# Filler products in TensorE's waits and four output buffers, in the tail of an attention and expert kernel

## The chip, the cores and the metric

One core of a Trainium2 chip. The metric is the device time of one execution in microseconds (us). The engines are TensorE (PE, its weight loads PEld), VectorE (DVE), ScalarE (ACT), GpSimd (POOL) and SyncE (SP), which issues DMAs.

## The reference

For 8 sequences of 512 tokens with 128 features: a modulated layer norm, causal attention with 16 heads and relative positions, a gated residual; then a second modulated layer norm and a layer of 16 experts, in which each token goes to one:

```python
x = x + ga * attention(layernorm(x) * (1 + ca) + sa)
h = (layernorm(x) * (1 + cb) + sb).reshape(-1, 128)
score = softmax(h @ Wg + bg)
gate, idx = max(score), argmax(score)
pos = rank of the token among those of its expert, in token order
keep = pos < 256                          # 4096 tokens / 16 experts
buf[idx, pos] = h                         # kept tokens alone
y = relu(buf @ W1 + b1) @ W2 + b2         # expert by expert
x = x + gb * where(keep, y[idx, pos] * gate, 0)
```

## The kernel before

Attention runs over 64 steps (8 sequences by 8 pairs of heads), one order written out by hand for each engine; the engines meet only at semaphores. A sequence's way into the experts lies inside the steps of the next one. For the last sequence it has no cover, and stands behind the steps as the tail: `project_out` (L729), the residual (`hn`, L1014), `turn_a` (transposes, L737), the layer norm of VectorE and GpSimd, `turn_h` (transposes, L744), ScalarE's `h2T`, `logits` (L750), the choice of the expert on VectorE, `places` (ranks by products, L757 to L762), indices, and four scatters of rows by GpSimd into a buffer in DRAM (L359). Each of these steps waits for the one before. A row of that buffer holds the token's normed values, its residual, its gate and its number (3 x 128 + 1 floats).

Meanwhile SyncE has loaded the weights of eight experts. It then waits for the scatters and loads the rows of experts 0 to 3 into four slots. From there on it waits for `ym` (TensorE done with expert e) and loads the weights of expert e + 8, and for `y` (output e summed) and loads the rows of expert e + 4.

TensorE does, for each expert e: `hidden(e)` (12 products with 256 columns, L850, on a high and a low part of both operands), `turn_e(e + 1)` (two transposes, L841) and `down(e)` (16 product instructions, L861, tile 0 and then tile 1 of 128 tokens, both in bank 6 or 7). `hidden(0)` needs `xhi` of ScalarE and `xlo` of VectorE (`low_x`). ScalarE does two of an expert's four relus, VectorE the other two (L1205).

VectorE's order for expert e is: `relu(e)`, `low_x(e + 1)`, `output(e - 1)`, `low_w1(e + 2)` (the low part of the weights, L1192). `output` waits until the scatter of the expert two before has left its buffer (`ysc`), converts the token numbers to indices (`yidx`, L1213), waits for `ym`, and sums: bias (L1217), times gate (L1219), plus residual (L1220), over both tiles at once. There are two output buffers, halves of the tile `row`. GpSimd then scatters the two tiles of each expert's output to their tokens (L414). Ahead of the experts, VectorE waits for the scatters of L359 and for the biases, and then does `low_w1` of experts 0 and 1 and `low_x(0)`.

In the names, `bank` is a bank of PSUM; `prb[0]` is bank 4, last read ahead of the last `weighted` (L722). `wohi` is the output projection's weight.

Of the kernel before, what the change touches and what calls it, by code (L numbers as in the profile page):

```python
# [32 lines left out]
U32 = mybir.dt.uint32  # L33
ALU = mybir.AluOpType
# [3 lines left out]
P = 128  # L38
B, S, D = 8, 512, 128
# [5 lines left out]
E, FF = 16, 512  # L45
# [25 lines left out]
def program(nc, x_d, qkv_d, qb_d, pos_d, wo_d, bo_d, wg_d, bg_d, w1_d, b1_d, w2_d, b2_d, c_d, wmod_d,  # L71
            consts_d, ktab_d, out_d):
    ctx = ExitStack()
    with ctx:
        def sb(name, shape, dt=F32):
            return ctx.enter_context(nc.sbuf_tensor(name, shape, dt))

        def sem(name):
# [86 lines left out]
        ye = row[:, :, 0:D].rearrange("p (a t) d -> p a t d", a=2)  # L165
        yidx = sb("yidx", [P, 2, ST], U32)
# [14 lines left out]
                 "xl0 xl1 xl2 xl3 w0 w1 w2 w3 w4 w5 w6 w7 w1h w1l tx xt xl hm hr hh2 ym y yi ysc0 ysc1").split()  # L181
# [18 lines left out]
        def waits(eng, *pairs):  # L200

            for name, value in pairs:
                wait(eng, name, value)

        def batches(turn):

            for b in range(B):
                turn(b, b == 0, b == B - 1)
# [5 lines left out]
        def one(tile, b, *rest):  # L214

            return tile[(slice(None), bass.ds(b, 1)) + rest]

# [4 lines left out]
        def _(sp):  # L222
# [72 lines left out]
            for e in range(E - 4):  # L295
                if e < E - 8:
                    sp.wait_ge(s["ym"], e + 1)
                    load_w1(e + 8, e)
                    load_w2(e + 8, e)
                sp.wait_ge(s["y"], e + 1)  # L300
                rows(e + 4, e % 4)
# [3 lines left out]
        def _(gp):  # L305
# [105 lines left out]
            def expert(e, par):  # L411
                waits(gp, ("pch", 1), ("y", e + 1), ("yi", e + 1))
                for t in range(ST):
                    gp.indirect_dma_start(out=out_d.rearrange("b s d -> (b s) d"),  # L414
                                          out_offset=bass.IndirectOffsetOnAxis(ap=yidx[:, par, t:t + 1], axis=0),
                                          in_=ye[:, par, t, :], in_offset=None,
                                          bounds_check=B * S - 1, oob_is_err=False).then_inc(s[f"ysc{par}"], 16)

            for e in range(E):
                expert(e, e % 2)  # L420
            for par in range(2):
                gp.wait_ge(s[f"ysc{par}"], 16 * ST * E // 2)
# [180 lines left out]
        def _(pe):  # L603
# [129 lines left out]
            def turn_a(b):  # L733

                pe.wait_ge(s["ga"], b)
                for q in range(QT):
                    last = pe.transpose(xtb[:, q * P:(q + 1) * P], hn[:, q * P:(q + 1) * P], ident)  # L737
                last.then_inc(s["t_a"], 1)
# [84 lines left out]
            pe.wait_ge(s["kt"], 4)  # L823
            batches(turn)
# [3 lines left out]
            weighted(NJ - 1, PAIRS - 1, NJ, 3)  # L828
            project_out(NJ - 1, PAIRS - 1)
            turn_a(B)  # L830
            pe.wait_ge(s["x2"], B)
            turn_h(B)
            logits(B)
            pe.wait_ge(s["lge"], B)
            places(B)

# [17 lines left out]
            def down(e, r):  # L854

                pe.wait_ge(s["hh2"], 2 * e + 1)
                for t in range(ST):
                    for n in range(NB):
                        if t == 0:
                            pe.wait_ge(s["hr" if n % 2 == 0 else "hh2"], 2 * e + n // 2 + 1)  # L860
                        last = pe.matmul(bank[6 + r % 2][:, t * P:(t + 1) * P], hid[:, r % 2, n, t * P:(t + 1) * P],  # L861
                                         w2[:, r, n, :], start=(n == 0), stop=(n == NB - 1))
                last.then_inc(s["ym"], 1)
# [17 lines left out]
        def _(dve):  # L881
# [326 lines left out]
            def output(e, r, first=False):  # L1208
                par = r % 2
                if not first:  # L1210
                    dve.wait_ge(s[f"ysc{par}"], 16 * (e - par))

                dve.tensor_copy(yidx[:, par, :], slots[:, r, :, 3 * D]).then_inc(s["yi"], 1)  # L1213
                dve.wait_ge(s["ym"], e + 1)

                rows = ye[:, par, :, :]
                link(dve.tensor_tensor(rows, bank[6 + par][:, 0:CAP].rearrange("p (t d) -> p t d", t=ST),  # L1217
                                       one(b2, e, slice(None)).to_broadcast([P, ST, D]), ALU.add))
                link(dve.tensor_tensor(rows, rows, slots[:, r, :, 2 * D:3 * D], ALU.mult))  # L1219
                dve.tensor_tensor(rows, rows, slots[:, r, :, D:2 * D], ALU.add).then_inc(s["y"], 1)  # L1220

            dve.wait_ge(s["scat"], 64 * B)
            dve.wait_ge(s["b2"], 16)
            for e in range(2):
                low_w1(e, e)
            low_x(0, 0)

            def expert(e, r, first=False):

                par = r % 2  # L1230
                relu(e, par)
                if e + 1 < E:
                    low_x(e + 1, 1 - par)
                if e:
                    output(e - 1, (r - 1) % 4, first)
                if e + 2 < E:
                    low_w1(e + 2, par)

            for e in range(E):
                expert(e, e % 4, e < 3)  # L1240
            output(E - 1, 3)


# [41 lines left out]
```

## Time and profile before

| | |
|---|---|
| median of 3 runs | 917.59 us (914.37, 918.48, 917.59) |
| profiled execution | 917.26 us, span 915.2 us |
| mean granted clock of TensorE | 0.972 |
| busy: PE, PEld | 94%, 75% of the span |
| busy: DVE, ACT, POOL | 73%, 78%, 57% of the span |
| chain of waits | PE 88%, DVE 5%, DMA 2%, ACT 2% |

A granted clock of 1.00 is 2.4 GHz, and 0.50 is 1.2 GHz. The span runs from the first to the last instruction. The attention steps end at about 812 us, the first rows are loaded at 839.9, the last scatter starts at 907.2. In a timeline a row can stand for several instructions of one kind (x4), and the time given is that of all of them; a product's time includes its way through the array, so that one starts before the last has ended.

### The profile page before, as it was taken

To read this page: it belongs to the slowest core of one execution; us is meant where nothing else is said; L and a number is where in the kernel's file an instruction comes from. 1 tells how busy PE (TensorE), PEld (TensorE's weight loads), DVE (VectorE), ACT (ScalarE), POOL (GpSimd) and SP (SyncE) were. 2 spreads that over 40 slices of the span, in tenths; PEclk is the share of its full clock that TensorE was granted. 3 is DMA by queue.
4 is the path that set the end of the run, shared out by engine and by line. 5 is a ranking of instruction groups with operands and counts; after the bars stand their busy time and mean duration, and the time that the engine had idled before them with its cause. 6 is when DMAs were issued, how large, how long until landed. Compare 5 with 4: busy or idle time off the path is not lost.

```text
span 915.2 us, 17265 instructions
## 1 busy us (share of the span) xinstructions
PE 857.6 (94%) x5453; PEld 686.8 (75%) x5453; DVE 667.8 (73%) x2051; ACT 710.9 (78%) x1966; POOL 519.6 (57%) x783
## 2 busy tenths in 40 slices
PE   5799999999999999999999999999999999963994
PEld 4577778777777787777777787777777877732994
DVE  5677778786878778777878787868787686743784
ACT  3688888888888888888888888888888888831441
POOL 3355555666556755675557556665567556732454
PEclk8899999999999999999999999999999999985997
DMA  8059000000000000000000000000000000025761
GB/s 247 1 163 257 19 1 13 1 1 36 13 2 1 36 1 13 1 19 17 13 1 15 12 14 1 1 21 12 2 1 21 1 13 1 13 72 165 224 196 39
DMA packets 31130, 38.43 MB, mean 42 GB/s; under 512 B 2982, under 2 KB 25703, under 8 KB 30784
## 3 DMA queue, kind: packets, MB, share of 16 engines
q1 hardware_dynamic: 27488, 29.69, 11.5%
q0 software_dynamic: 3072, 5.94, 1.8%
q10 hardware_dynamic: 480, 1.70, 0.5%
q8 instruction: 44, 0.72, 0.3%
q14 instruction: 46, 0.38, 0.1%
HBM read 22.97 MB, written 16.82 MB: 43 GB/s over the span
## 4 chain that ended last, share of the span: by engine, by line
PE 88%; DVE 5%; DMA 2%; ACT 2%; issue 1%; POOL 1%; SPq 0%; POOLq 0%; DVEq 0%
PE bank L694 22%; PE bank L659 16%; PE bank L722 16%; PE bank L702 15%; PE bank L729 5%; PE bank L680 5%; PE bank L691 3%; PE bank L861 2%; PE bank L850 2%; DMA out<-row,yidx 1%; ACT prob L493 1%; PE bank L750 1%; DVE xn L930 1%; DMA small<-in_L_ffn_b 1%; PE bank L744 0%
## 5 line engine op out<-in xcount | busy, mean ns | idle before, releaser
L373 POOL TENSOR_SCALAR prob<-prob,rsum 128x128 f32<-128x128 f32 (+3 forms) x512 | 263.7, 534 | 238.1 <-DVE rsum L987 233.6
L493 ACT ACTIVATE prob<-srow,nmax 128x512 f32<-128x512 f32 (+3 forms) x512 | 286.2, 560 | 66.7 <-DVE nmax L975 64.0
L975 DVE CUSTOM_DVE_ANT_0 srow<-bank,consts 128x512 f32<-128x512 f32 (+3 forms) x512 | 246.7, 489 | 100.0 <-issue 78.6
L702 PE MATMUL bank<-consts,prob 128*128 128x128 f32 x1280 | 201.9, 272 | 0.2 <-POOL prob L373 0.2
L702 PEld LDWEIGHTS bank<-consts,prob 128*128 128x128 f32 x1280 | 158.6, 140 | 23.3 <-POOL prob L373 0.5
L366 POOL TENSOR_TENSOR qlo<-qx,qhi 128x384 fp32r<-128x384 f32 x128 | 129.9, 1015 | 58.1 <-ACT qhi L482 57.3
L502 ACT ACTIVATE pt<-bank 128x384 f32<-128x384 f32 x318 | 153.6, 496 | 5.5 <-PE bank L702 5.0
L722 PE MATMUL bank<-pt,v 128*64 128x512 f32 (+3 forms) x1024 | 152.0, 439 | 0.2 <-issue 0.2
L694 PE MATMUL bank<-khi,qhi 128*128 128x512 f32 (+2 forms) x384 | 145.9, 380 | 5.9 <-DVE wolo L1175 2.4
L992 DVE SCALAR_TENSOR_TENSOR qx<-bank,qbias,consts 128x512 f32<-128x512 f32 x128 | 94.1, 735 | 53.6 <-PE bank L659 53.4
L694 PE MATMUL bank<-khi,qlo 128*128 128x512 f32 (+2 forms) x384 | 130.2, 339 | 0.0
L694 PE MATMUL bank<-klo,qhi 128*128 128x512 f32 (+2 forms) x384 | 128.9, 336 | 0.0
L722 PEld LDWEIGHTS bank<-pt,v 128*64 128x64 f32 x1024 | 68.0, 136 | 76.8 <-issue 59.6
L998 DVE SCALAR_TENSOR_TENSOR klo<-bank,khi 64x512 fp32r<-64x512 f32 x128 | 87.8, 686 | 18.9 <-ACT kx L477 16.8
L493 ACT ACTIVATION_READ_ACCUMULATOR prob<-srow,nmax 128x1 f32 x512 | 97.5, 191 | 0.0
L482 ACT ACTIVATE qhi<-qx 128x384 fp32r<-128x384 f32 x128 | 66.6, 520 | 38.1 <-DVE qx L992 37.6
L659 PE MATMUL bank<-hhi,whi 128*128 128x512 f32 x189 | 86.5, 458 | 1.0 <-DVE qx L992 0.9
L694 PEld LDWEIGHTS bank<-khi,qhi 128*128 128x128 f32 x384 | 72.2, 188 | 19.6 <-issue 6.9
L694 PEld LDWEIGHTS bank<-klo,qhi 128*128 128x128 f32 x384 | 72.8, 190 | 7.7
L476 ACT ACTIVATE khi<-bank 64x512 fp32r<-64x512 f32 x128 | 75.2, 588 | 2.7 <-PE bank L659 1.2
L694 PEld LDWEIGHTS bank<-khi,qlo 128*128 128x128 f32 x384 | 72.2, 188 | 5.4
L659 PE MATMUL bank<-hhi,wlo 128*128 128x512 f32 x189 | 74.7, 395 | 0.0
(166 smaller groups left out, 1388.4 us busy)
## 6 DMA issues: line engine op xcount, KB each, us to landing
xbuf<-fill SPq DMA_DIRECT2D x4, 1540.0 KB, 23.2
x<-xbuf SPq DMA_DIRECT2D x16, 385.0 KB, 3.4
raw<-in_L_ffn_W SPq DMA_DIRECT2D x16, 256.0 KB, 8.7
prob<-in_L_ffn_W SPq DMA_DIRECT2D x16, 256.0 KB, 4.8
out<-row SPq DMA_DIRECT2D x8, 256.0 KB, 2.3
raw<-in_L_attn_qkv ACTq DMA_DIRECT2D x3, 512.0 KB, 5.9
modb<-mod_rows SPq DMA_DIRECT2D x1, 1536.0 KB, 8.1
v<-in_L_ffn_b SPq DMA_DIRECT2D x1, 1024.0 KB, 6.9
```

Of the source, the lines that this page charges most:

```text
L366: gp.tensor_tensor(qlo[:, h, :], qx[:, h, P:S], qhi[:, h, :], ALU.subtract).then_inc(s["ql"], 1)
L373: end = gp.tensor_scalar(part, part, rsum[:, par, 4 * h + q:4 * h + q + 1], 1.0, ALU.mult, ALU.mult)
L476: act.activation(khi[0:HD, h, :], prb[0][h * HD:(h + 1) * HD, :], ACT.Copy, scale=C_QKV)
L493: act.activation(prob[:, par, h, QOFF[q]:QOFF[q] + P * (q + 1)], srow[:, k % 4, 0:P * (q + 1)], ACT.Exp, bias=nmax[:, par, k:k + 1], scale ...
L502: act.activation(pt[:, h, KOFF[g]:KOFF[g] + GW[g]], source[:, 0:GW[g]], ACT.Copy)\
L659: last = pe.matmul(out, w[:, a, cols], h, start=(i == 0), stop=(i == 2))
L694: last = pe.matmul(out, a[:, h, (q - 1) * P:q * P], b[:, h, 0:P * (q + 1)], start=(i == 0), stop=(i == 2))
L702: last = pe.transpose(out[:, n * P:(n + 1) * P], prob[:, par, h, QOFF[q] + k * P:QOFF[q] + (k + 1) * P], ident)
L722: last = pe.matmul(otb[h * HD:(h + 1) * HD, k * P:S], v[:, g, k, at + h * HD:at + (h + 1) * HD], pt[:, h, KOFF[k]:KOFF[k] + S - k * P], st ...
L975: dve.tensor_tensor_reduce(out=srow[:, k % 4, 0:w], in0=scb[k % 2][:, 0:w], in1=mask[:, S - w:S], scale=-1.0, scalar=BIG, op0=ALU.add, op1 ...
L992: dve.scalar_tensor_tensor(qx[:, h, :], prb[h][:, :], qbias[:, h, a:a + 1], qtab, ALU.add, ALU.mult).then_inc(s["qe"], 1)
L998: dve.scalar_tensor_tensor(klo[0:HD, h, :], prb[0][h * HD:(h + 1) * HD, :], C_QKV, khi[0:HD, h, :], ALU.mult, ALU.subtract).then_inc(s["kl ...
```

## The change

The diff adds `idle(n)`: n products of `wohi` with 512 of its own columns into `prb[0]`, without a wait or a signal. They stand in TensorE's order in the tail: 6 before the last `project_out`, 4 before `turn_a`, 14 before `turn_h`, 3 before `logits`, 6 before `places`, 44 behind `places`.

The expert outputs get four buffers (`ye`, two in `row` and two in `xh`), with four scatter semaphores; `output` waits for the scatter of the expert four before. `ym` and `y` are now raised once per tile. GpSimd waits for each tile by itself before it scatters it. `output` can do one tile alone; that of expert 15 is summed and scattered tile by tile, its second tile coming from bank 0 in place of bank 7. `output(14)` stands before `relu(15)`, no longer behind it. `low_w1` of experts 0 and 1 stands before the wait for the scatters.

```diff
--- before.py
+++ after.py
@@ -162,8 +162,8 @@
         xf = x[:, :, :].rearrange("p t d -> p (t d)")
         slots = xf[:, 0:4 * ST * RW].rearrange("p (a t w) -> p a t w", a=4, t=ST)
         hid = srow[:, :, :].rearrange("p k s -> p (k s)").rearrange("p (a n c) -> p a n c", a=2, n=NB)
-        ye = row[:, :, 0:D].rearrange("p (a t) d -> p a t d", a=2)
-        yidx = sb("yidx", [P, 2, ST], U32)
+        ye = [row[:, 0:2, 0:D], row[:, 2:4, 0:D], xh[:, 0:2, :], xh[:, 2:4, :]]
+        yidx = sb("yidx", [P, 4, ST], U32)
 
         bank = [ctx.enter_context(nc.psum_tensor(f"bank{i}", [P, 512], F32)) for i in range(8)]
         scb, trb, prb, otb, opb = bank[0:2], bank[2:4], bank[4:6], bank[6], bank[7]
@@ -178,7 +178,7 @@
                  "st1 st2 rst1 rs1 xn t_x hn vhi vlo hld wv qh ql kl kt wos ol ga t_a "
                  "sc tt ex rc nm tr evA evB pv oe qp qe kp ke vp ve op "
                  "dch pch va1 va2 x2 rst2 rs2 xh h2a h2 t_h hh lg lge lm lex oh gate gg pre prx idx scat filled x2st "
-                 "xl0 xl1 xl2 xl3 w0 w1 w2 w3 w4 w5 w6 w7 w1h w1l tx xt xl hm hr hh2 ym y yi ysc0 ysc1").split()
+                 "xl0 xl1 xl2 xl3 w0 w1 w2 w3 w4 w5 w6 w7 w1h w1l tx xt xl hm hr hh2 ym y yi ysc0 ysc1 ysc2 ysc3").split()
         s = {n: sem("s_" + n) for n in names}
 
         class Chain:
@@ -214,6 +214,10 @@
         def one(tile, b, *rest):
 
             return tile[(slice(None), bass.ds(b, 1)) + rest]
+
+        def down_bank(e, t):
+
+            return bank[0] if (e, t) == (E - 1, ST - 1) else bank[6 + e % 2]
 
         block = ctx.enter_context(nc.Block())
 
@@ -294,10 +298,10 @@
                 rows(e, e)
             for e in range(E - 4):
                 if e < E - 8:
-                    sp.wait_ge(s["ym"], e + 1)
+                    sp.wait_ge(s["ym"], ST * (e + 1))
                     load_w1(e + 8, e)
                     load_w2(e + 8, e)
-                sp.wait_ge(s["y"], e + 1)
+                sp.wait_ge(s["y"], ST * (e + 1))
                 rows(e + 4, e % 4)
 
 
@@ -408,18 +412,19 @@
             scatter(B, range(QT))
 
 
-            def expert(e, par):
-                waits(gp, ("pch", 1), ("y", e + 1), ("yi", e + 1))
+            def expert(e, r):
+                waits(gp, ("pch", 1), ("yi", e + 1))
                 for t in range(ST):
+                    gp.wait_ge(s["y"], ST * e + t + 1)
                     gp.indirect_dma_start(out=out_d.rearrange("b s d -> (b s) d"),
-                                          out_offset=bass.IndirectOffsetOnAxis(ap=yidx[:, par, t:t + 1], axis=0),
-                                          in_=ye[:, par, t, :], in_offset=None,
-                                          bounds_check=B * S - 1, oob_is_err=False).then_inc(s[f"ysc{par}"], 16)
+                                          out_offset=bass.IndirectOffsetOnAxis(ap=yidx[:, r, t:t + 1], axis=0),
+                                          in_=ye[r][:, t, :], in_offset=None,
+                                          bounds_check=B * S - 1, oob_is_err=False).then_inc(s[f"ysc{r}"], 16)
 
             for e in range(E):
-                expert(e, e % 2)
-            for par in range(2):
-                gp.wait_ge(s[f"ysc{par}"], 16 * ST * E // 2)
+                expert(e, e % 4)
+            for r in range(4):
+                gp.wait_ge(s[f"ysc{r}"], 16 * ST * E // 4)
 
 
         @block.scalar
@@ -821,18 +826,30 @@
             pe.wait_ge(s["ve"], 3)
             pe.wait_ge(s["ktab"], 48)
             pe.wait_ge(s["kt"], 4)
+            def idle(n):
+
+                for _ in range(n):
+                    pe.matmul(prb[0][:, :], wohi[:, 0, :], wohi[:, 0:4, :].rearrange("p a d -> p (a d)"),
+                              start=True, stop=True)
+
             batches(turn)
             for i in range(6):
                 transpose_group(free[i], NJ - 1, 1, *divmod(i, 3))
             project_out(NJ - 2, PAIRS - 2)
             weighted(NJ - 1, PAIRS - 1, NJ, 3)
+            idle(6)
             project_out(NJ - 1, PAIRS - 1)
+            idle(4)
             turn_a(B)
+            idle(14)
             pe.wait_ge(s["x2"], B)
             turn_h(B)
+            idle(3)
             logits(B)
+            idle(6)
             pe.wait_ge(s["lge"], B)
             places(B)
+            idle(44)
 
 
             def turn_e(r):
@@ -858,9 +875,9 @@
                     for n in range(NB):
                         if t == 0:
                             pe.wait_ge(s["hr" if n % 2 == 0 else "hh2"], 2 * e + n // 2 + 1)
-                        last = pe.matmul(bank[6 + r % 2][:, t * P:(t + 1) * P], hid[:, r % 2, n, t * P:(t + 1) * P],
+                        last = pe.matmul(down_bank(e, t)[:, t * P:(t + 1) * P], hid[:, r % 2, n, t * P:(t + 1) * P],
                                          w2[:, r, n, :], start=(n == 0), stop=(n == NB - 1))
-                last.then_inc(s["ym"], 1)
+                    last.then_inc(s["ym"], 1)
 
             pe.wait_ge(s["prx"], B)
             pe.wait_ge(s["xl0"], 16)
@@ -1205,40 +1222,35 @@
                     dve.tensor_scalar(hid[:, par, n, :], bank[2 + n][:, 0:CAP], smallT[:, bass.ds(16 + NB * e + n, 1)],
                                       0.0, ALU.add, ALU.max).then_inc(s["hh2"], 1)
 
-            def output(e, r, first=False):
-                par = r % 2
-                if not first:
-                    dve.wait_ge(s[f"ysc{par}"], 16 * (e - par))
-
-                dve.tensor_copy(yidx[:, par, :], slots[:, r, :, 3 * D]).then_inc(s["yi"], 1)
-                dve.wait_ge(s["ym"], e + 1)
-
-                rows = ye[:, par, :, :]
-                link(dve.tensor_tensor(rows, bank[6 + par][:, 0:CAP].rearrange("p (t d) -> p t d", t=ST),
-                                       one(b2, e, slice(None)).to_broadcast([P, ST, D]), ALU.add))
-                link(dve.tensor_tensor(rows, rows, slots[:, r, :, 2 * D:3 * D], ALU.mult))
-                dve.tensor_tensor(rows, rows, slots[:, r, :, D:2 * D], ALU.add).then_inc(s["y"], 1)
-
+            def output(e, t0=0, t1=ST):
+                r, width = e % 4, (t1 - t0) * P
+                if t0 == 0:
+                    wait(dve, f"ysc{r}", 32 * (e // 4))
+                    dve.tensor_copy(yidx[:, r, :], slots[:, r, :, 3 * D]).then_inc(s["yi"], 1)
+                dve.wait_ge(s["ym"], ST * e + t1)
+                rows = ye[r][:, t0:t1, :]
+                link(dve.tensor_tensor(rows, down_bank(e, t0)[:, t0 * P:t1 * P].rearrange("p (t d) -> p t d", d=D),
+                                       one(b2, e, slice(None)).to_broadcast([P, t1 - t0, D]), ALU.add))
+                link(dve.tensor_tensor(rows, rows, slots[:, r, t0:t1, 2 * D:3 * D], ALU.mult))
+                dve.tensor_tensor(rows, rows, slots[:, r, t0:t1, D:2 * D], ALU.add).then_inc(s["y"], t1 - t0)
+
+            for e in range(2):
+                low_w1(e, e)
             dve.wait_ge(s["scat"], 64 * B)
             dve.wait_ge(s["b2"], 16)
-            for e in range(2):
-                low_w1(e, e)
             low_x(0, 0)
 
-            def expert(e, r, first=False):
-
-                par = r % 2
-                relu(e, par)
-                if e + 1 < E:
-                    low_x(e + 1, 1 - par)
+            for e in range(E - 1):
+                relu(e, e % 2)
+                low_x(e + 1, 1 - e % 2)
                 if e:
-                    output(e - 1, (r - 1) % 4, first)
+                    output(e - 1)
                 if e + 2 < E:
-                    low_w1(e + 2, par)
-
-            for e in range(E):
-                expert(e, e % 4, e < 3)
-            output(E - 1, 3)
+                    low_w1(e + 2, e % 2)
+            output(E - 2)
+            relu(E - 1, 1)
+            for t in range(ST):
+                output(E - 1, t, t + 1)
 
 
 def host_constants():
```

## Rows read from the trace of the kernel before

**Rows 1.** Stretches: length, busy us (x instructions) of PE, PEld, DVE, ACT, POOL; clock.

```profile
52.30:55.70 3.40, 1.84 (x14) 0.96 (x10) 3.30 (x16) 1.26 (x5) 0.08 (x1) 1.00 0.02 4
813.40:816.80 3.40, 1.61 (x7) 0.90 (x7) 1.50 (x3) 0.00 (x0) 0.00 (x0) 1.00 0.00 0
816.90:821.30 4.40, 0.00 (x0) 0.00 (x0) 2.66 (x13) 0.00 (x0) 1.29 (x2) 0.50 0.69 194
841.70:847.50 5.80, 5.75 (x27) 5.78 (x28) 2.08 (x4) 1.85 (x4) 0.00 (x0) 0.50 0.22 78
```

**Rows 2.** Timeline of the tail: start, us, instruction, count, [idle before it <- releaser].

```profile
813.85 0.50 PE L729 MATMUL bank<-ohi,wohi 128*128 128x512 f32 x1 [1.42 <-DVE olo L1004]
...
815.82 0.66 PE L737 MATMUL bank<-consts,hn 128*128 128x128 f32 x4 [1.00 <-DVE hn L1014]
...
821.34 1.09 PE L744 MATMUL bank<-consts,xh 128*128 128x128 f32 x4 [4.87 <-DVE xh L1037]
823.29 1.89 PE L750 MATMUL bank<-wg,h2T 128*128 128x16 f32 x8 [0.87 <-ACT h2T L512]
826.87 0.21 PE L757 MATMUL bank<-oh,upper 128*128 128x64 bf16 x1 [1.69 <-DVE oh L1061]
...
836.94 1.29 DVE L1192 TENSOR_TENSOR wlo<-raw,whi 128x512 fp32r<-128x512 f32 x2 [7.36 <-DMA xbuf<-row,sidx]
...
840.07 0.66 PE L841 MATMUL bank<-consts,x 128*128 128x128 f32 x2 [12.80 <-DMA x<-xbuf]
841.75 0.55 PE L850 MATMUL bank<-hhi,whi 128*128 128x256 f32 x1 [1.02 <-DVE hlo L1199]
```

**Rows 3.** Timeline of TensorE earlier in the run, both levels of the clock.

```profile
25.62 0.63 PE L659 MATMUL bank<-vhi,whi 128*128 128x512 f32 x1
26.05 0.63 PE L659 MATMUL bank<-vlo,whi 128*128 128x512 f32 x1
...
28.77 0.40 PE L680 MATMUL bank<-wvhi,vlo 128*128 128x512 f32 x1
29.00 0.40 PE L680 MATMUL bank<-wvhi,vhi 128*128 128x512 f32 x1
...
171.05 0.60 PE L744 MATMUL bank<-consts,xh 128*128 128x128 f32 x4
...
182.46 0.96 PE L750 MATMUL bank<-wg,h2T 128*128 128x16 f32 x8
```

**Rows 4.** Timeline of TensorE, first product of experts 1, 6, 7, 10, 11, 15.

```profile
847.87 0.36 PE L850 MATMUL bank<-hhi,whi 128*128 128x256 f32 x1
...
865.25 0.36 PE L850 MATMUL bank<-hhi,whi 128*128 128x256 f32 x1
...
869.71 0.36 PE L850 MATMUL bank<-hhi,whi 128*128 128x256 f32 x1
...
880.31 0.37 PE L850 MATMUL bank<-hhi,whi 128*128 128x256 f32 x1
...
884.78 0.36 PE L850 MATMUL bank<-hhi,whi 128*128 128x256 f32 x1
...
898.72 0.37 PE L850 MATMUL bank<-hhi,whi 128*128 128x256 f32 x1
```

**Rows 5.** Waits behind 845: who for whom, us in total, times, longest us.

```profile
DVE yidx L1213 <- DMA out<-row,yidx: 3.5, 4, 1.4
```

**Rows 6.** Timeline of GpSimd and VectorE at the end.

```profile
900.09 0.97 POOL L414 DMA_INDIRECT out<-row,yidx  x1 [1.14 <-DVE row L1220]
901.36 0.97 POOL L414 DMA_INDIRECT out<-row,yidx  x1 [0.30 <-DVE yidx L1213]
...
903.64 0.45 DVE L1213 CAST yidx<-x 128x2 uint32<-128x2 f32 x1 [1.36 <-DMA out<-row,yidx]
...
907.17 0.97 POOL L414 DMA_INDIRECT out<-row,yidx  x1 [0.30 <-issue]
```

**Rows 7.** VectorE's groups behind 845: count, busy us, mean ns, idle before.

```profile
L1205 DVE TENSOR_SCALAR srow<-bank,smallT 128x256 f32<-128x256 f32 x31 | 14.7, 481 | 5.1 <-PE bank L850 4.7
L1219 DVE TENSOR_TENSOR row<-row,x 128x256 f32<-128x256 f32 x16 | 6.9, 429 | 0.5
```

## Prediction

> **What bounds the kernel now.** I read the table of busy shares first: TensorE is busy 94% of the span and 88% of the chain of waits runs through it, so the attention stage, which the change does not touch, is TensorE's. What the change can move lies behind that stage: about 812 to 915 us. There the windows show the granted clock. It is 1.00 up to 816.8, although TensorE is busy for only 1.61 of the last 3.4 us, 0.50 right behind, and still 0.50 while the first expert runs [rows 1]. The timeline of TensorE shows why: from the last output projection on, each short group of products waits for another engine, 1.42, 1.00, 4.87, 0.87, 1.69 and then 12.80 us, and the chain goes through VectorE, GpSimd and a DMA and back each time [rows 2]. The tail is thus a latency chain with TensorE as one link, and every TensorE link behind 816.9 runs at 1.2 GHz in place of 2.4 GHz. From 841.75 on it is TensorE's again: sixteen experts, one after the other.
>
> All sums are made against the profiled execution: 917.26 us, of which 915.2 is the span. It lies 0.3 us under the median of 917.59; the three runs differ by 4.1 us, nearly as much as I come to forecast.
>
> **Step 1, the filler itself.** At full clock a product with 512 columns starts 0.23 us after the one before (28.77, 29.00), at half clock 0.43 us (25.62, 26.05) [rows 3]. The fillers have this shape, write a bank that nobody reads any more, and wait for nothing. At full clock they are, in order, 6 x 0.23 = 1.4 us into a slot of 1.42; 4 = 0.9 into 1.00; 14 = 3.2 into 4.87; 3 = 0.7 into 0.87; 6 = 1.4 into 1.69; 44 = 10.1 into 12.80 [rows 2]. They all fit, so their cost is nothing, and the cover is those waits. If the cover is gone (half clock) they need 2.6, 1.7, 6.0, 1.3, 2.6 and 18.9 us, and TensorE takes its instructions in order: the next transpose or product is late by the excess, and with it VectorE's routing, the scatters and the rows' DMA.
>
> **Step 2, the links before the rows are loaded.** Four transposes took 1.09 us at 821.34 and 0.60 at 171.05; the eight products of the logits 1.89 at 823.29 and 0.96 at 182.46 [rows 2, 3]. With the clock kept that is 0.5 + 0.9 us earlier, and an estimated 0.15 for the small products of the places: 1.6 in all. Will it be kept? Fall and no fall have a row each. Busy 1.61 of 3.4 us, the clock fell right behind it; busy 1.84 of 3.4 us (52.3 to 55.7), it stayed at 1.00 [rows 1]. In the new tail the leanest stretch is from the end of the fourteen (about 819.5) to the start of the logits (822.8): 1.8 us idle, 0.6 of transposes, 0.7 of filler, and nothing for 0.1. That is nearer to the row behind which it fell. I take the transposes' 0.5 whole, since a fall can hardly come before them, half of the logits' 0.9, and 0.1 of the places': **1.1 us**. The ends: 1.6; and 0 where the clock falls ahead of the logits, since six fillers at half clock (2.6) overrun their slot by 0.9, which eats most of what the transposes gave.
>
> The Trainium skill speaks to this point ("TensorE: Matmul & The Clock Gate", section "Why this matters for your kernels"): what it warns of is one long idle gap between bursts, not a sum of short ones. This trace disagrees: the clock fell at 816.9 behind gaps of only 1.42 and 1.00 us [rows 2]. By the page nothing in the new tail would cost the clock; that is the first rival below.
>
> **Step 3, the first experts.** The last filler ends near 835.6; the rows of expert 0 then land near 838.4 (1.6 us earlier than now). So TensorE idles for some 2.8 us, does two transposes (0.66 now, an estimated 0.4 warm, by the ratio of step 2), and idles for 1.0 again while the two halves of x are made. That is leaner than either row of [rows 1]. So the clock is likely to fall once more, but late, having been full until then, and it comes back during expert 0 or 1. Now it is half for all of 841.7 to 847.5 [rows 1], which costs 6.12 us from the start of expert 0 (841.75) to that of expert 1 (847.87) in place of an undisturbed 3.49 (worked out in step 4): 2.6 us [rows 2, 4]. The ends are 0 and 2.6; no row says when the fall comes, so I take the middle, **1.2 us**, and **0.2** for the transposes.
>
> **Step 4, four output buffers.** From expert 1 to expert 15, 14 intervals take 898.72 - 847.87 = 50.85 us; two are 869.71 - 865.25 = 4.46 and 884.78 - 880.31 = 4.47, the other twelve average 3.49 [rows 4]. In both long ones VectorE stood at the conversion of the indices until the scatter of the expert two before had landed (four such waits, 3.5 us, the longest 1.4 [rows 5]), and behind it stood the relu for which TensorE waits. With four buffers it waits for the expert four before, seven us older. Both stalls go: 8.93 - 6.98 = **1.9 us**. What would be late next is TensorE itself (its intervals are full); the loads of rows and weights are asked for three and eight experts ahead, as now. Ends: 0.9 (one stall comes back, as the queue of loads is as full as before) and 1.9.
>
> **Step 5, the residue products ahead of the scatter wait.** They ran 1.29 us from 836.94, and nobody needed them before 841.75; VectorE had been idle for 7.36 us before [rows 2]. Moved into that idle time they save 0. The cover of both places is the scatters and the load of the rows; without it 1.3 us would be at stake.
>
> **Step 6, the end.** Now the scatter of expert 13 starts at 900.09 and 901.36, one per 1.27 us, and the last one at 907.17, behind an output that waited 1.36 us for its buffer at 903.64 [rows 6]; from there to the end of the span are 8.0 us, which stay. In the new order output 14 (three operations of 0.43) goes before the two relus of expert 15 (0.48 each) [rows 7]: these come 0.7 us later, and so do expert 15's down products, until about 903. Its second tile is then summed by about 904.1. But GpSimd has four scatters behind 901.36, one every 1.27: the last starts at 901.36 + 4 x 1.275 = 906.46, and it, not the sum, is late. Gain 907.17 - 906.46 = **0.7 us**. Ends: if each wait ahead of a single tile costs the 0.8 us that now lie between an output and its scatter, -1.4; if GpSimd were quicker than its rows, the sum would set the end at 905.2, +1.9. Two more semaphores to wait for at the very end and one more signal per expert of TensorE I put at nothing: no row has them as a wait.
>
> **Sum.** 1.1 + 1.2 + 0.2 + 1.9 + 0.7 = 5.1 us; 917.26 - 5.1 = **912.2 us**, 0.6% under the median.
>
> **Rivals.** *A. The clock is kept throughout*: 1.6 + 2.6 + 0.3 + 1.9 + 0.7 = 7.1, so **910.2 us**. For it: between 812 and 836 TensorE is then nearly always busy. Against it: the idle 2.8 + 1.0 us in front of expert 0.
> *B. The filler does nothing for the time*: the clock falls near 822 and is half again where the first experts run; only the buffers and the end are left, 2.6 us, so **914.7 us**. For it: the fall behind a stretch with 1.61 of 3.4 us busy. Against it: the long run of 44 products, as dense as the nine of 25 to 28 us, behind which the clock had risen [rows 3].
> *C. Slower: the fillers run at half clock.* The overruns are 1.1 (fourteen), 0.4 (three), 0.9 (six) and 6.1 us (forty-four): 8.5 us late, less the 2.6 of buffers and end, **923.2 us**. It decides from this point: the forty-four take 10.1 us plus 0.47 for each us at half clock, and fill 12.80 when 5.8 us of them are half; with the 2.4 us of overruns before, the change is a loss from about 6.2 us on. Against it: at 841.75 the clock was back 5.8 us after dense work began, and in the first dense stretch within 4.
> *D. The buffers don't help*, as the stalls come from elsewhere: 1.9 less, **914.1 us**. Against it: the releaser in the row is the scatter's DMA.
>
> **How the numbers follow.** What a measurement of this kernel can tell from no change is about 0.5%, 4.6 us: under 913.0 is faster, over 922.2 slower. Chances: the forecast case (910.8 to 913.9) 0.50, A 0.20, B 0.18, C 0.04, D or a mix of B and D 0.08. The forecast case lies under 913.0 in three of four, so faster is 0.20 + 0.37 = 0.57; same 0.13 + 0.18 + 0.07 = 0.38; slower 0.05, C and some misfortune. The likeliest case has 910.8 to 913.9; for 8 in 10 the range reaches to A less the 1 us by which a median of such runs moves, and to B with the same: 909.2 to 915.7.
>
> **What would show it.** The page's clock row at 1.0 up to about 838 (steps 1, 2); the logits' eight products at 0.96 us; expert 0 to expert 1 between 3.5 and 6.1 us (step 3); no wait for the scatter's DMA at the index conversion and no interval over 4 us (step 4); six last scatters at 1.27 us with no gap (step 6). The prediction is wrong if a filler is still running when its successor's input is there, or if the clock at expert 0 is as it was.

## The result, and the profile after

The changed kernel takes 914.45 us (median of 13 runs, 912.86 to 917.08) against 917.59 us: a ratio of 0.9973 with a 95% interval of 0.9962 to 0.9983. It is 0.27% faster, 2.5 us by the ratio. The forecast was 912.2 us and 5.1 us less. The medians themselves are 3.1 us apart. The time lies inside the forecast range, but the gain is about half of the forecast.

The profiled execution took 913.59 us, 3.7 us less than that of before; its span is 911.8 us. That is one execution, better than the median of its kernel. Its windows over the tail show the length of each stretch, the busy time of PE, PEld, DVE, ACT and POOL, the granted clock, and then the share of the DMA engines and their GB/s:

```profile
816.80:821.20 4.40, 2.73 (x13) 1.93 (x12) 2.61 (x13) 0.00 (x0) 1.29 (x3) 1.00 0.69 198
823.90:827.10 3.20, 3.20 (x16) 2.21 (x16) 1.93 (x10) 1.29 (x3) 1.04 (x1) 0.50 1.17 329
827.30:840.70 13.40, 10.20 (x46) 7.96 (x45) 2.72 (x10) 0.38 (x1) 4.14 (x4) 1.00 0.42 136
840.90:844.20 3.30, 3.30 (x17) 3.30 (x17) 0.97 (x2) 1.26 (x4) 0.00 (x0) 0.50 0.50 178
```

Where the clock was 0.50 from 816.9 to past 847.5 [rows 1], it now falls twice, each time for some 3.4 us: once at 823.8, while the six fillers ahead of the places run, and once at 840.9, just as expert 0 starts. The timeline of TensorE in the tail shows what each fall costs:

```profile
821.19 0.63 PE L749 MATMUL bank<-consts,xh 128*128 128x128 f32 x4 [1.67 <-DVE xh L1054]
...
822.69 1.07 PE L755 MATMUL bank<-wg,h2T 128*128 128x16 f32 x8 [0.17 <-ACT h2T L517]
823.60 2.75 PE L832 MATMUL bank<-wohi 128*128 128x512 f32 x6
826.15 0.28 PE L762 MATMUL bank<-oh,upper 128*128 128x64 bf16 x1
...
826.47 10.61 PE L832 MATMUL bank<-wohi 128*128 128x512 f32 x44
839.14 0.41 PE L858 MATMUL bank<-consts,x 128*128 128x128 f32 x2 [2.07 <-DMA x<-xbuf]
840.68 0.40 PE L867 MATMUL bank<-hhi,whi 128*128 128x256 f32 x1 [1.12 <-DVE hlo L1216]
```

The transposes and the logits run at full clock (0.63 and 1.07 us, where they took 1.09 and 1.89 [rows 2]). Then six fillers take 2.75 us, and the places start only when they have drained, at 826.15; the choice they need was written at 825.30. More than half of the 1.26 us won until then goes there.

The first products of experts 1, 5, 6, 9, 10 and 15 answer to [rows 4]:

```profile
845.65 0.36 PE L867 MATMUL bank<-hhi,whi 128*128 128x256 f32 x1
...
859.75 0.37 PE L867 MATMUL bank<-hhi,whi 128*128 128x256 f32 x1
...
863.59 0.36 PE L867 MATMUL bank<-hhi,whi 128*128 128x256 f32 x1
...
874.18 0.37 PE L867 MATMUL bank<-hhi,whi 128*128 128x256 f32 x1
...
878.10 0.36 PE L867 MATMUL bank<-hhi,whi 128*128 128x256 f32 x1
...
895.80 0.37 PE L867 MATMUL bank<-hhi,whi 128*128 128x256 f32 x1
```

Expert 0 takes 845.65 - 840.68 = 4.97 us, 1.15 less. Experts 1 to 15 take 50.15 us, only 0.70 less than 50.85. The two intervals of 4.46 us are gone, but there are two of 3.84 and 3.92 (from 859.75 and 874.18), and the other twelve average 3.53, not 3.49. In the first of the two, the load of the rows is asked for at 856.92, and TensorE's weight load waits for it (SyncE's queue, then PEld):

```profile
856.92 0.37 SPq L255 DMA_DIRECT2D x<-xbuf  x1
...
861.61 0.20 PEld L858 LDWEIGHTS bank<-consts,x 128*128 128x128 f32 x2 [0.40 <-DMA x<-xbuf]
```

VectorE no longer waits for a scatter; in the list of waits the transposes' wait for the rows stands in its place (us in total, times, longest):

```profile
PEld bank L858 <- DMA x<-xbuf: 0.9, 2, 0.5
```

And the last scatters on GpSimd, which answer to [rows 6]:

```profile
897.22 0.97 POOL L419 DMA_INDIRECT out<-row,yidx  x1 [1.16 <-DVE yidx L1229]
898.50 0.97 POOL L419 DMA_INDIRECT out<-row,yidx  x1 [0.30 <-issue]
899.77 1.07 POOL L419 DMA_INDIRECT out<-xh,yidx  x1 [0.30 <-issue]
901.14 0.97 POOL L419 DMA_INDIRECT out<-xh,yidx  x1 [0.30 <-issue]
...
903.70 0.97 POOL L419 DMA_INDIRECT out<-xh,yidx  x1 [0.30 <-issue]
```

They now follow each other without a gap. From the first product of expert 15 to the end of the span are 911.8 - 895.80 = 16.0 us, against 915.2 - 898.72 = 16.5.

The whole difference of the two profiled executions, 3.67 us: attention 0.2, links of the tail 0.8 (from the start of the last copy of the attention output on ScalarE, `ohi`, 812.48 before and 812.31 after, to the first transpose of expert 0: 27.59 to 26.83 us), transposes and halves of expert 0 0.1, expert 0 1.15, experts 1 to 15 0.7, the end 0.5, outside the span 0.2.

### The profile page after: what moved, and what is told of

Read it like the earlier page. It is cut to its first block, busy times and chain, and to the rows that moved or that the text cites. A ratio compares the mean times of both kernels' runs of the same rounds, so it can differ in the third digit from the quotient of the medians.

```text
span 911.8 us, 17438 instructions
## 1 busy us (share of the span) xinstructions
PE 874.1 (96%) x5530; PEld 699.3 (77%) x5530; DVE 667.1 (73%) x2054; ACT 710.9 (78%) x1966; POOL 518.9 (57%) x783
## 3 DMA queue, kind: packets, MB, share of 16 engines
HBM read 22.97 MB, written 16.82 MB: 44 GB/s over the span
## 4 chain that ended last, share of the span: by engine, by line
PE 89%; DVE 4%; DMA 2%; ACT 2%; issue 1%; POOL 1%; SPq 0%; POOLq 0%; DVEq 0%
PE bank L699 22%; PE bank L664 16%; PE bank L727 16%; PE bank L707 15%; PE bank L734 5%; PE bank L685 5%; PE bank L696 3%; PE bank L878 2%; PE bank L867 2%; ACT prob L498 1%; DMA x<-xbuf 1%; PE bank L755 1%; DVE xn L947 1%; DMA small<-in_L_ffn_b 1%; PE bank L832 0%
```

## The experiments

Below, "e0" is the time from the first product of expert 0 to that of expert 1, and "e1-15" from there to that of expert 15. They come from one profiled execution each; the ratios are to the kernel before on the same chip, with 95% intervals. Two kernels were run once and have a time in place of a ratio.

| kernel | ratio | e0 | e1-15 | to the end |
|---|---|---|---|---|
| before | 1 | 6.12 | 50.85 | 16.5 |
| changed | 0.9973 (0.9962 to 0.9983) | 4.97 | 50.15 | 16.0 |
| e1_no_filler | 0.9980 (0.9971 to 0.9989) | 6.20 | 50.33 | 16.2 |
| e2_filler_only | 0.9986 (0.9976 to 0.9996) | 5.60 | 51.22 | 16.8 |
| e8_two_buffers | 0.9991 (0.9982 to 1.0001) | 6.06 | 51.46 | 16.4 |
| e7_light_before | 0.9973 (0.9964 to 0.9982) | 5.10 | 48.79 | 16.8 |
| e3_light_loads | 0.9950 (0.9936 to 0.9964) | 5.01 | 49.18 | 15.9 |
| e4_spread_loads | 0.9963 (0.9950 to 0.9975) | 4.97 | 49.38 | 15.9 |
| e5_fill_to_rows | 0.9939 (0.9927 to 0.9951) | 3.44 | 50.83 | 16.0 |
| e12_twenty | 0.9969 (0.9957 to 0.9981) | 6.07 | 49.63 | 16.0 |
| e11_one_signal | 0.9977 (0.9968 to 0.9986) | 5.01 | 50.30 | 15.9 |
| e9_together | 0.9938 (0.9924 to 0.9951) | 3.44 | 49.27 | 16.2 |
| e6_old_order | 913.21 us | 3.44 | 49.82 | 16.3 |
| e10_double_last | 918.73 us | 3.43 | 49.33 | 15.9 |

**One part alone.** e1_no_filler:

```diff
-            idle(6) ... idle(4) ... idle(14) ... idle(3) ... idle(6) ... idle(44)
```

> The changed kernel with none of the 77 filler products; all else stays. Theory: the filler is worth about 2.1 us (0.8 in the links of the tail, 0.1 in the transposes of expert 0, 1.15 between expert 0 and expert 1), and the buffers and the end about 1.1, so this kernel takes about 916.5 us, ratio to the kernel before 0.9988, and its clock is 0.50 from about 817 to past 845. Rival (the filler does nothing for the time): the same as the changed kernel, ratio 0.997.

e2_filler_only is the kernel before with `idle` and its six calls.

> The kernel before with the 77 filler products alone. Theory: ratio about 0.9977 (2.1 us less); expert 0 to expert 1 about 5.0 us, and the two long intervals of about 4.47 us at experts 6 and 10 are still there. Rival: ratio 1.000.

Without the filler 1.8 us are left of the gain, with the filler alone 1.3; the two sum to 3.1. The interval of e2_filler_only stays just clear of 1, so the filler alone does shorten the run. The sizes are less sure: each ratio is good to about 0.9 us either way, which leaves room for the 2.1 us that the profiles gave the filler and for my 1.1 for buffers and end, and the changed kernel is only 0.6 us better than the one without filler, with overlapping intervals. The long intervals of e2_filler_only were there, as expected, but at experts 4 and 8 (4.77 and 4.52 us), not 6 and 10, and expert 0 took 5.60 us, not 5.0. With the filler alone the clock was 1.00 from 813 to 839, with no fall at the logits, and 0.5 in front of and through expert 0:

```profile
813.00:839.00 26.00, 21.44 (x104) 16.30 (x104) 9.56 (x34) 2.66 (x5) 8.83 (x9) 1.00 0.54 164
839.30:846.00 6.70, 5.59 (x26) 5.25 (x27) 2.45 (x5) 2.23 (x5) 0.00 (x0) 0.51 0.45 139
```

e8_two_buffers takes the four buffers back and keeps the rest. The lines that matter (indices, scatters and semaphores go with them):

```diff
-        ye = [row[:, 0:2, 0:D], row[:, 2:4, 0:D], xh[:, 0:2, :], xh[:, 2:4, :]]
+        ye = [row[:, 0:2, 0:D], row[:, 2:4, 0:D]]
-                    wait(dve, f"ysc{r}", 32 * (e // 4))
+                    wait(dve, f"ysc{e % 2}", 32 * (e // 2))
```

> The changed kernel with two output buffers in place of four (filler, per-tile signals and the end kept). Theory: the waits of VectorE's index conversion for the scatters are back, experts 1 to 15 take about 51.2 us (50.85 to 51.2 in the kernel before and with the filler alone, 0.2 to 0.4 more if the signal per tile is what makes every other interval 3.59 in place of 3.53), ratio 0.9985. Rival (the buffers only moved the wait and bring nothing): 50.2 us, ratio 0.997.

The wait for the scatters came back, intervals of 4.70 and 4.53 with it, and e1-15 rose to 51.46 us. The ratio is 0.0018 above that of the changed kernel: 1.7 us, with the two intervals just touching. So in the new code the four buffers are worth 1.3 us of e1-15 by the profiles and 1.7 us by the times. From its list of waits:

```profile
DVE yidx L1229 <- DMA out<-row,yidx: 2.9, 3, 1.0
```

**What is late once the buffers are four.** e3_light_loads, and e7_light_before the same edit in the kernel before, leave out all but 4 KB of each W2 of experts 8 to 15, so that their output is wrong and only the times count (the added line is cut short at "..."):

```diff
-                    load_w2(e + 8, e)
+                    sp.dma_start(w2[0:8, e, 0:1, :], w2_d[e + 8][0:8]. ...).then_inc(s[f"w{e}"], 16)
```

> The changed kernel, but of W2 of experts 8 to 15 only 4 KB each are loaded (experts 8 to 15 then use stale values; half of the weight traffic behind expert 0 is left out). Theory: in the changed kernel what makes intervals of 3.84 and 3.92 us is that the rows of expert e + 4 are asked for when output e is summed, about 4.9 us before they are transposed, and land late while weights are being loaded. With light loads they land in under 3.6 us, no interval is over 3.65, expert 1 to expert 15 takes about 49.2 us in place of 50.15, ratio 0.996. Rival (VectorE's order or the per-tile signals set the interval): 50.1 us as now, ratio 0.997.

> The kernel before with the same light loads of W2. Theory: its two intervals of 4.46 us come from scatters that land late behind the weight loads, so they go too: expert 1 to expert 15 takes about 49 us in place of 50.85, ratio 0.998. Rival (two buffers are too few at any DMA load): the long intervals stay, ratio 1.000.

The intervals and e1-15 came out as the theory said. First products of experts 1 and 15 in the changed kernel and in the kernel before, both with light loads:

```profile
845.78 0.36 PE L868 MATMUL bank<-hhi,whi 128*128 128x256 f32 x1
...
894.96 0.37 PE L868 MATMUL bank<-hhi,whi 128*128 128x256 f32 x1
```

```profile
847.26 0.36 PE L851 MATMUL bank<-hhi,whi 128*128 128x256 f32 x1
...
896.05 0.37 PE L851 MATMUL bank<-hhi,whi 128*128 128x256 f32 x1
```

With light loads no interval is over 3.65 in either. Two buffers are enough then (48.79), and four are no better (49.18). For two buffers that is clear: e1-15 was 50.85, 51.22 and 51.46 us in the three profiles with all loads. So the weight loads on the DMA engines make the output scatters late there. For four buffers it is less so, since a long interval does not come in every execution: with all loads, asked for as in the changed kernel, seven profiles have e1-15 between 49.33 and 50.83 us, and the one of 49.33 (e10_double_last) has no interval over 3.66 either. What points to the loads is the wait for the rows. TensorE's weight loads waited for rows in six of these seven profiles, for 0.4 to 1.7 us in all, and not with light loads. A wait on the rows shows with the buffers and no filler too, and is longer than in the changed kernel:

```profile
PE bank L852 <- DMA x<-xbuf: 1.0, 1, 1.0
```

That is from the waits of e1_no_filler, where it makes one interval of 4.65 us.

e4_spread_loads leaves nothing out; it asks for the same weights over half as long again:

```diff
-                if e < E - 8:
+                if e % 3 < 2:
+                    n = e // 3 * 2 + e % 3
                     sp.wait_ge(s["ym"], ST * (e + 1))
-                    load_w1(e + 8, e)
-                    load_w2(e + 8, e)
+                    load_w1(n + 8, n)
+                    load_w2(n + 8, n)
```

> The changed kernel, but the weights of experts 8 to 15 are asked for behind experts 0, 1, 3, 4, 6, 7, 9, 10 in place of 0 to 7, so that the same bytes are spread over half as long again. Nothing is left out. Theory (the rows' loads are late behind the weights' loads): no interval over 3.7 us, expert 1 to 15 about 49.3 us, 0.9 us less than the changed kernel, ratio 0.996. Rival (any full load of weights delays a row load that falls on it): 50.1 us, ratio 0.997.

In the profile it did what it should: no interval over 3.66, e1-15 49.38, 0.77 less than the changed kernel. The ratio is 0.0010 lower than the changed kernel's, which the intervals can't tell from none, and e10_double_last had as few long intervals without the edit.

**The clock at expert 0.** e5_fill_to_rows:

```diff
-            idle(44)
+            idle(52)
...
             turn_e(0)
+            idle(4)
```

> The changed kernel with 52 fillers in place of 44 behind the places, and 4 more between the transposes of expert 0 and its products. Theory: the clock falls near 840 since TensorE is idle for 2.1 and 1.1 us there; with the gaps filled it stays at 1.00, expert 0 takes 3.5 us in place of 4.97, ratio 0.9955. Rival (a fall comes all the same, as transposes and small products weigh nothing, or the fillers now overrun the rows): expert 0 still takes 4.9 us or more, ratio 0.997 to 0.9985.

The granted clock stayed at 1.00 from 813 to 904 us, and expert 0 took 844.58 - 841.14 = 3.44 us:

```profile
813.00:904.00 91.00, 81.21 (x599) 73.83 (x596) 59.43 (x163) 31.06 (x67) 39.88 (x41) 1.00 0.58 173
```

```profile
839.61 0.41 PE L858 MATMUL bank<-consts,x 128*128 128x128 f32 x2 [1.06 <-DMA x<-xbuf]
839.78 1.17 PE L832 MATMUL bank<-wohi 128*128 128x512 f32 x4
841.14 0.36 PE L867 MATMUL bank<-hhi,whi 128*128 128x256 f32 x1 [0.20 <-DVE hlo L1217]
...
844.58 0.36 PE L867 MATMUL bank<-hhi,whi 128*128 128x256 f32 x1
```

Twelve more fillers are worth 0.0034, about 3 us, the largest step of the study and more than the whole change. The two intervals don't meet. The profiles show only a part of it: 1.5 us at expert 0 and 0.4 us between the last copy and the first transpose (26.45 us in place of 26.83). Where the rest comes from is not shown. Nor is it shown which of the two groups, the eight or the four, keeps the clock.

e12_twenty (20 for 14 ahead of the transposes of the second norm):

> The changed kernel with 20 fillers in place of 14 ahead of the transposes of the second norm. Theory: with the idle 1.67 us there gone the clock doesn't fall at the logits in any run, the places come at +13.13 us behind the last copy of the attention output in place of +13.84, and the rows 0.45 earlier in the runs that had the fall: ratio 0.9965 against 0.997. Rival (the overrun of fillers makes the transposes late): transposes later than +8.88, ratio 0.9975.

The transposes were not late (they start 8.89 us behind the start of the last copy, where they had started 8.88), and the places came 13.14 us behind it. But six of the eight other kernels of the study with 14 there had no fall at the logits either, so one profile shows little, and the ratio none. In that profile the clock was half for nearly all of expert 0 (6.07 us).

e10_double_last (88 for 44), one run:

> The changed kernel with 88 fillers in place of 44 in the last group. Theory: the fillers have no cover behind the rows' landing; the last of them starts 44 x 0.232 = 10.2 us later, at about 847, so the first transposes of expert 0 come 7.9 us later than at 839.1, and the clock is then 1.00 at expert 0 (1.5 us back): 6.4 us more than the changed kernel, about 920 us. Rival (TensorE lets what is ready pass the fillers): no change, 914 us.

```profile
826.68 20.22 PE L832 MATMUL bank<-wohi 128*128 128x512 f32 x88
846.74 0.38 PE L858 MATMUL bank<-consts,x 128*128 128x128 f32 x2
848.24 0.35 PE L867 MATMUL bank<-hhi,whi 128*128 128x256 f32 x1 [1.12 <-DVE hlo L1216]
```

It took 918.73 us, 5.1 us more than the profiled execution of the changed kernel, where 6.4 were expected. The first transposes stood behind all 88 fillers, 7.6 us later than in the changed kernel; expert 0 gave back 1.5 us and experts 1 to 15, with no late rows, 0.8. Here no product passed the fillers, and they cost what they reach beyond the end of the wait.

**The end.** e6_old_order, one run (913.21 us):

```diff
-            for e in range(E - 1):
+            for e in range(E):
                 relu(e, e % 2)
...
-            output(E - 2)
-            relu(E - 1, 1)
```

> The changed kernel with the relus of expert 15 ahead of output 14 again, the last expert still tile by tile. Theory: down 15 ends about 0.7 us earlier but output 14 comes about 1.0 later, so that GpSimd, which sets the end, stands idle before the scatters of expert 14; from expert 15's first product to the end of the span 16.4 us in place of 16.0. Rival (the order is free): 16.0.

16.3 us to the end: GpSimd stands idle for 0.57 us in place of 0.30 in front of the first scatter of expert 14 (899.52), and the scatter before takes 1.16:

```profile
897.79 1.16 POOL L419 DMA_INDIRECT out<-row,yidx  x1 [0.30 <-issue]
899.52 0.97 POOL L419 DMA_INDIRECT out<-xh,yidx  x1 [0.57 <-issue]
...
903.36 0.97 POOL L419 DMA_INDIRECT out<-xh,yidx  x1 [0.30 <-issue]
```

So the order is worth 0.3 to 0.4 us in this profile (16.34 against 15.95), as expected, too little for the time. The clock of this run fell at 823 and was back at 1.00 from 829.8 on; it did not fall again at expert 0 (e0 3.44). Part of its 44 fillers had run at half clock, so that they ended later, and TensorE was idle for only 1.54 us before the rows landed, where the changed kernel had 2.07:

```profile
840.28 0.41 PE L858 MATMUL bank<-consts,x 128*128 128x128 f32 x2 [1.54 <-DMA x<-xbuf]
```

**The signal per tile.** e11_one_signal:

```diff
-                    last.then_inc(s["ym"], 1)
+                    if t == ST - 1 or e == E - 1:
+                        last.then_inc(s["ym"], 1)
```

> The changed kernel with one signal of TensorE per expert for experts 0 to 14, and two for expert 15. Theory: every other interval goes from 3.59 back to 3.53 us, 0.4 us in all over experts 1 to 15, too little for the time (ratio 0.997 or 0.9965). Rival (the four buffers make it): intervals as they are.

The theory fell: every other interval is still 3.59. The rival, the four buffers, had fallen with e8_two_buffers, whose intervals show 3.59 as well. What makes the changed expert code some 0.03 us per expert slower (48.79 against 49.18 with light loads, 14 intervals) stays open; the wait of GpSimd for each tile was not tried alone.

**Together.** e9_together has e5's, e12's, e4's and e11's edits:

> The changed kernel with four edits together: 20 fillers in place of 14, 52 in place of 44 and 4 between the transposes and the products of expert 0; the weights of experts 8 to 15 spread over eleven experts; the signal per tile only for expert 15. Theory: clock 1.00 through the whole tail, expert 0 takes 3.44 us, experts 1 to 15 about 48.9 us with no interval over 3.65, so 1.9 us less than with the longer filler alone, ratio 0.992. Rival (the gains overlap, as a late expert 0 had given the loads time): experts 1 to 15 take 50 us, ratio 0.994.

911.85 us, ratio 0.9938: the same as with e5's edit alone (911.73 us, 0.9939), and the rival's ratio, not the 0.992 of the theory. The clock was 1.00 through the tail up to 901 us, e0 3.44 and e1-15 49.27, between the 48.9 of the theory and the rival's 50. The rest of the edits brought nothing that the time shows. e5's profiled execution had e1-15 at 50.83, with one interval of 5.2 us behind late rows, but it was the slowest of that kernel's six runs (913.19); how often such an interval comes in the other runs is not known. Its wait:

```profile
PE bank L858 <- DMA x<-xbuf: 1.5, 1, 1.5
```

## Why the prediction was wrong, step by step

**Step 1, the filler fits into the waits: right at full clock.** The fillers start 0.23 us apart, and the fourteen left the 1.67 us of idle time that follow from the sum. Where the clock fell, the places came 0.85 us behind the choice, in place of 0.14 before, so the six overran by 0.7 us (0.9 was given). e10_double_last shows the price of an overrun.

**Step 2, the links: 1.1 forecast, 0.8 in the profile.** The profile mixes the two ends: transposes and logits were at full clock (1.26 us gained by the time of the choice), then the fall came and took 0.7 of it back. In e2, e3, e5, e8, e10 and e11 there was no fall and the scatters started 1.25 us earlier than before, counted from the last copy; in e4 and e6 there was one, and in e6 the scatters came 0.15 us later than before. The middle was fair; that the fall comes in three of these nine profiles was not to be read from the rows.

**Step 3, expert 0: 1.2 + 0.2 forecast, 1.15 + 0.1 measured.** The mechanism was right: the clock falls once more in front of expert 0, as the fillers end too early. The number is luck: it was the middle between two ends for want of a row, and other profiles of the same fillers lie at both ends. Over the kernels that keep the 44 fillers, e0 was 3.44 to 6.07 us; in the three without any filler it was 5.10 to 6.20. In front of it TensorE was idle for 1.54 us where e0 was 3.44, for 2.07 and 2.15 where it was 4.97, and for 2.8 to 3.0 where it was 5.0 to 6.1. With e5_fill_to_rows expert 0 took 3.44 us, so another 1.5 us was left there.

**Step 4, four buffers: 1.9 forecast, 0.7 measured. This is the step that failed most clearly**, in the sentence "What would be late next is TensorE itself ... the loads of rows and weights are asked for three and eight experts ahead". The weights are; the rows are not. They are asked for when output e is summed, which is near the start of expert e + 2, and are transposed behind the first products of expert e + 3: 4.7 us later (856.92 to 861.61), where the twelve loads behind 845 us take 3.6 us to land in the median and 4.7 at most. Before, the stall on the scatters seems to have given them time: in the three profiles with two buffers and all loads, TensorE's weight loads waited for rows for 0.3 us or not at all. With the stall gone the rows are late behind the same weight loads, and 0.7 of the 1.94 us of the two stalls come back as waits for rows (3.84 + 3.92 - 2 x 3.53); another 0.5 us is lost in 0.04 us per expert (3.53 against 3.49), whose cause stays open. With half of the weight traffic left out, the kernel before gains with its two buffers what I had forecast for four (2.1 us). The 0.7 is the difference of two single profiles: over all profiles with all loads asked for as before, e1-15 averages 51.2 us with two buffers (three) and 50.1 with four (seven), so 1.1 us is the better figure for the buffers' gain, still well under 1.9.

**Step 5: right.** The residue products ran at 828.51, at once behind the indices, and neither the scatters nor the first products of expert 0 moved for it: the scatters start 16.82 us behind the last copy in e2_filler_only, which has the residue products behind its wait, and 16.83 in e8_two_buffers, which has them ahead. It was not tried alone.

**Step 6, the end: 0.7 forecast, 0.5 measured.** GpSimd sets the end, as said, one scatter per 1.27 us; one took 1.37 and the first began 0.05 later. The 905.2 of the upper end was not worked out from a row; nothing hung on it.

**The sum.** In the profile the terms of steps 2 to 6 are 3.3 us in place of 5.1, and 1.2 of the missing 1.8 is step 4. The median moved less than the profiled executions (2.5 to 3.1 us), as the one of the changed kernel lies 0.9 us under its median. The times divide the shortfall otherwise than the profiles: of the 2.5 us forecast for the filler they show 1.3 (e2_filler_only) or 0.6 (the changed kernel against e1_no_filler), and of the 2.6 for buffers and end 1.8. Each is good to about 0.9 us, so by the times the filler's steps fell short too, by an amount that stays open. None of the rivals is what happened. B (914.7 us) and D (914.1) come nearest to the median of 914.45 in their time, but not in their cause. Against B ("the filler does nothing"), e2_filler_only is faster than the kernel before. Against D ("the buffers don't help"), the stalls did come from the scatters' DMA, and another transfer took part of their place. A did not happen: the clock fell twice. C's overruns were the 0.7 us of the six alone. One reading under C was a little off: in the first dense stretch the clock was back 4.2 us after the first product (24.20 to 28.39), not within 4.

## What to carry to other kernels

When a wait on a DMA is taken away by another buffer, ask for each other transfer on the same engines how long ahead of its use it is issued, in us from two rows, and not how many buffers ahead it is; where the DMA engines were nearly full, as here (0.95 of their time busy from 852 to 860 us), the wait moved to the load with the least slack. Fillers for the clock should reach up to the work that is to be fast: here twelve more products in the last short idle times in front of it were worth more (3 us) than the first seventy-seven (0.6 to 1.3). They must end before the wait does, since no product passed them here.

## What the runs showed of the hardware

The same 77 fillers left the clock at 1.00 from 813 to 839 us in e2_filler_only and let it fall at 823.8 in the changed kernel, with nearly the same idle time before the transposes (1.65 and 1.67 us): whether a lean stretch costs the clock is not the same in each run. At expert 0 the fall cost between nothing and 2.6 us (e0 from 3.44 to 6.07).

It does not follow that the clock makes the 4 us by which runs of one kernel differ (912.86 to 917.08 in the changed kernel). The slowest of its thirteen runs had a mean granted clock of 0.987, as high as any of them, and the five runs of e3_light_loads lie within 1.0 us and the eleven of e11_one_signal within 1.3, though the profiles of both have the clock at half for most of expert 0. Two parts that do differ between profiles are the start of the last copy of the attention output (812.31 to 813.51 us), though no edit changes what the engines do ahead of it, and the long intervals of experts 1 to 15. What moves the first was not looked into.
